# Performer attention layer, last batch: feature buffers of their own for two query groups, and a new order of the closing stages

## The reference, cut to what matters

```
feature_map(y): (exp(y @ orf.T / 32**0.25 - |y|^2 / (2 sqrt(32))) + 1e-6) / sqrt(128)    # per head, 16 heads of 32
q, k = feature_map(x Wq^T + bq), feature_map(x Wk^T + bk);   v = x Wv^T + bv
kv = k^T v;  ksum = sum over tokens of k;   out = (q kv) / (q ksum)
x = layernorm(x + out Wo^T + bo)
x = layernorm(x + x (ternary(weight) * scale)^T)
```

## Time and profile before

| | us |
|---|---|
| median of 3 runs | 1277.04 (1276.66 to 1277.28) |
| the profiled execution | 1281.79 |
| its span in the trace | 1280.0 |
| TensorE busy | 1257.8 (98%) |
| VectorE, ScalarE, GpSimd busy | 901.4, 712.4, 359.1 |
| mean granted TensorE clock | 0.996 of full speed |

### The profile page before, as it was taken

One profiled execution on the slowest core, in us unless ns is written; L12 is line 12 of the kernel. 1 busy time (PEld: TensorE's weight loads), 2 busy tenths in 40 slices (PEclk: granted clock), 3 DMA queues, 4 the chain that ended last, 5 costly groups with the idle time before them and its releaser, 6 DMA issues.

```text
span 1280.0 us, 24908 instructions
## 1 busy us (share of the span) xinstructions
PE 1257.8 (98%) x8626; PEld 961.0 (75%) x8626; DVE 901.4 (70%) x1615; ACT 712.4 (56%) x1435; POOL 359.1 (28%) x745
## 2 busy tenths in 40 slices
PE   9999999999999999999999999999999999999986
PEld 8767688777877678776787778876788777886665
DVE  6589665796658865688657877578765686657666
ACT  5657445574366743667337763477544674355534
POOL 0113342124321333213422134312342133421143
PEclk9999999999999999999999999999999999999899
DMA  7658304773146811576215761268603774046611
GB/s 240 152 135 216 97 34 122 178 197 83 54 118 170 209 54 58 139 178 175 62 58 139 193 166 55 62 157 203 158 25 85 173 191 130 34 114 143 152 34 66
DMA packets 82748, 160.32 MB, mean 125 GB/s; under 512 B 17856, under 2 KB 36416, under 8 KB 82112
## 3 DMA queue, kind: packets, MB, share of 16 engines
q1 hardware_dynamic: 68880, 139.78, 43.8%
q10 hardware_dynamic: 9648, 16.85, 3.5%
q0 software_dynamic: 4096, 2.11, 0.7%
HBM read 39.13 MB, written 16.78 MB: 44 GB/s over the span
## 4 chain that ended last, share of the span: by engine, by line
PE 88%; DVE 2%; ACT 1%; DMA 1%; issue 1%; SPq 1%; POOL 1%; ACTq 0%; POOLq 0%; DVEq 0%
PE ps L969 25%; PE ps L932 21%; PE ps L1033 9%; PE ps L982 8%; PE ps L987 5%; PE ps L1000 4%; PE ps L955 4%; PE ps L957 4%; PE ps L956 4%; PE ps L1059 2%; DMA rows<-in_x_t 1%; DMA stacks<-norm_rows 1%; PE ps L1009 1%; DVE stats L789 0%; SPq L534 0%
## 5 line engine op out<-in xcount | busy, mean ns | idle before, releaser
L691 ACT ACTIVATE features<-ps 128x512 f32<-128x512 f32 x512 | 277.8, 602 | 133.2 <-PE ps L982 127.3
L982 PEld LDWEIGHTS ps<-orf_stack,stacks 98*128 98x128 f32 x1024 | 131.3, 192 | 30.5 <-issue 21.3
L932 PE MATMUL ps<-Wo_hi,stacks 128*128 128x512 f32 x448 | 150.5, 402 | 0.0
L672 ACT ACTIVATE unit_hi<-ps,cols 128x512 fp32r<-128x512 f32 x128 | 88.5, 691 | 103.8 <-PE ps L969 103.8
L664 ACT ACTIVATE values_then_attention<-ps 128x512 f32<-128x512 f32 x64 | 38.2, 597 | 192.9 <-PE ps L957 190.8
L841 DVE SCALAR_TENSOR_TENSOR unit_lo<-ps,cols,unit_hi 128x512 fp32r<-128x512 f32 x128 | 94.0, 734 | 63.6 <-ACT squares L674 63.6
L583 POOL CAST norm_rows<-norms_turned 128x32 fp32r<-128x32 f32 x64 | 14.0, 219 | 439.9 <-DVE norms_turned L859 439.9
L805 DVE TENSOR_TENSOR den<-den,features 128x512 f32<-128x512 f32 x186 | 127.9, 688 | 11.5 <-ACT features L691 0.9
L982 PE MATMUL ps<-orf_stack,stacks 98*128 98x128 f32 x1024 | 130.9, 272 | 1.2 <-ACT features L691 1.1
L567 POOL TENSOR_SCALAR stats<-stats 128x1 f32<-128x1 f32 x128 | 36.0, 282 | 340.0 <-DVE stats L792 339.8
L1033 PE MATMUL ps<-features,kv_ksum 128*32 128x512 f32 x1024 | 123.1, 608 | 2.5 <-ACT kv_ksum L712 1.6
(11 more groups left out here) (132 smaller groups left out, 2598.6 us busy)
## 6 DMA issues: line engine op xcount, KB each, us to landing
stacks<-unit_hi SPq DMA_DIRECT2D x512, 128.0 KB, 2.4
stacks<-unit_lo SPq DMA_DIRECT2D x256, 128.0 KB, 2.7
out<-rows ACTq DMA_DIRECT2D x56, 256.0 KB, 2.0
rows<-in_x_t SPq DMA_DIRECT2D x49, 256.0 KB, 3.3
rows<-in_x SPq DMA_DIRECT2D x32, 256.0 KB, 4.0
features<-in_x SPq DMA_DIRECT2D x32, 256.0 KB, 3.7
values_then_attention<-in_x_t SPq DMA_DIRECT2D x8, 256.0 KB, 6.9
stacks<-norm_rows POOLq DMA_DIRECT2D x128, 16.0 KB, 2.6
```

The lines of the kernel that those rows point to most:

```text
L672: nc.scalar.activation(EH[:, u % 2, half], ps[:, :], ACT.Identity, bias=BC[:, u:u + 1]).then_inc(a_p.sem, 1)
L691: nc.scalar.activation(FE[:, n % 8, :, 0:M], ps[:, :].rearrange("p (a m) -> p a m", a=HG), ACT.Exp, scale=C_EXP).then_inc(a_exp.sem, 1)
L932: last = mm(out, a, b, start=(n == 0), stop=(n == len(terms) - 1))
L982: last = mm(ps[:, M * h:M * (h + 1)], slot[0:QK, L * h + P * r:L * h + P * (r + 1)], ORF[0:QK, h, :], start=True, stop=True)
```

## The change

It touches the last batch only. The query features of units 5 and 7 go to `own_buffers` (XR, X4, a new buffer of two tiles, and DR[:, 1]), not to FE. Unit 5 runs G2 ahead of F5.2 and P(7,1), and after F5.7 it goes F6.0, F6.1, GG2.0, GG2.1, R2.0, Q(7,1), N, LIFT, NL. Unit 6 has no G left. Unit 7 runs F7.0, F7.1, then all eight G3 tiles. All eight x rows load into FE once G3.7 is done. AG(0,1), AG(1,1), AG(2,1), A and GG3.1 move as shown. In the closing loop Y(t-1) stands ahead of ST(t-4), and SP issues the stores in place of ACT. `sums_on_pe` is unchanged.

```diff
 def split_at(b, g):
-    return 4 if sums_on_pe(b, g) else 0
+    return 0
+def has_own_buffers(b, u):
+    return b + 1 == B and u in (NU - 3, NU - 1)
...
     if is_key(u):
-        early = [("AG", b, 0, 0), ("AG", b, 1, 0)] if b + 1 == B and u + 2 == NU else []
+        if b + 1 == B and u + 2 == NU:
+            return f(2, 3, 4) + [("R", b, g - 1, 1), ("AG", b, 0, 0)] + f(5, 6, 7) + [("AG", b, 1, 0)]
...
         if b + 1 == B and u == NU - 3:
-            seq += p[1] + s0 + l0 + kv + f(2, 3) + p[2] + f(4, 5) + s1 + q0 + [("KVT", b, g)] + f(6, 7) + l1 + [("GG", b, g, 0)] + q1 + norm + lift
-            seq += [("GG", b, g, 1), ("R", b, g, 0)] + [("LR", b, t) for t in range(4)]
+            seq += kv + f(2, 3) + p[1] + [("KVT", b, g)] + q0 + f(4, 5) + p[2] + s1 + l1 + f(6, 7)
+            seq += [("F", b, u + 1, 0), ("F", b, u + 1, 1), ("GG", b, g, 0), ("GG", b, g, 1), ("R", b, g, 0)] + q1 + norm + lift
...
     if b + 1 == B:
-        seq = [("R", b, g - 1, 1), ("AG", b, 2, 0)] + f(0, 1, 2) + kv + [("AG", b, 0, 1)] + f(3) + [("OK", b, 0, 0)]
-        seq += [("KVT", b, g)] + f(4, 5) + [("AG", b, 1, 1), ("AG", b, 2, 1), ("A", b, 0), ("A", b, 1), ("OK", b, 0, 1), ("OK", b, 0, 2)]
-        seq += [("GG", b, g, 0), ("R", b, g, 0, 0), ("AG", b, g, 0, 0)] + f(6, 7) + [("OK", b, 1, k) for k in range(3)]
-        seq += [("R", b, g, 0, 1), ("AG", b, g, 0, 1), ("OK", b, 0, 3), ("LN", b, 0), ("OK", b, 1, 3), ("LN", b, 1), ("A", b, 2), ("A", b, 3)]
-        seq += [("GG", b, g, 1)] + [("OK", b, 2, k) for k in range(KT)] + [("LN", b, 2), ("Y", b, 0), ("A", b, 4)]
+        seq = f(0, 1) + kv + [("LR", b, t) for t in range(4)] + f(2, 3) + [("AG", b, 2, 0), ("OK", b, 0, 0), ("KVT", b, g)] + f(4, 5) + [("OK", b, 0, 1)] + f(6, 7)
+        seq += [("AG", b, 0, 1), ("OK", b, 0, 2), ("A", b, 0), ("A", b, 1), ("GG", b, g, 0), ("R", b, g, 0, 0), ("AG", b, g, 0, 0)]
+        seq += [("OK", b, 1, k) for k in range(3)] + [("R", b, g, 0, 1), ("AG", b, g, 0, 1), ("GG", b, g, 1)]
+        seq += [("OK", b, 0, 3), ("LN", b, 0), ("OK", b, 1, 3), ("LN", b, 1), ("AG", b, 1, 1), ("AG", b, 2, 1), ("A", b, 2), ("A", b, 3)]
+        seq += [("OK", b, 2, k) for k in range(KT)] + [("LN", b, 2), ("Y", b, 0), ("A", b, 4)]
...
-        seq += o(t, 3) + [("LN", b, t)] + (o(t + 1, 0, 1, 2) if t + 1 < TT else []) + [("YT", b, t - 2), ("ST", b, t - 4), ("Y", b, t - 1), ("FF", b, t - 3)]
+        seq += o(t, 3) + [("LN", b, t)] + (o(t + 1, 0, 1, 2) if t + 1 < TT else []) + [("YT", b, t - 2), ("Y", b, t - 1), ("ST", b, t - 4), ("FF", b, t - 3)]
...
+        own_buffers = [XR[:, r, :] for r in range(4)] + [X4[:, :], F2[:, 0, :], F2[:, 1, :], DR[:, 1, :]]
...
+                elif kind == "ST" and b + 1 == B:
+                    t = at[0]
+                    wait(a_out.sem, a_out.nth(b, t + 1))
+                    sp.dma_start(out_tiles[b, t], normed(b, t)).then_inc(d_st[t % 4].sem, 16)
```

More of the change, by code:

```diff
@@ L103, in unit_stages @@
         st = [[("ST", b - 1, t)] if u == 0 and b else [] for t in (TT - 2, TT - 1)]
-        half = [("G", b, g, r) for r in range(split_at(b, g))]
-        early = [("AG", b, 0, 0), ("AG", b, 1, 0)] if b + 1 == B and u + 2 == NU else []
+        if b + 1 == B and u + 2 == NU:
+            return f(2, 3, 4) + [("R", b, g - 1, 1), ("AG", b, 0, 0)] + f(5, 6, 7) + [("AG", b, 1, 0)]
         if u == 0:
-            seq = f(0, 1) + p[1] + s0 + l0 + f(2, 3) + q0 + st[0] + p[2] + f(4, 5) + half + s1 + l1 + f(6, 7) + q1 + norm + lift
+            seq = f(0, 1) + p[1] + s0 + l0 + f(2, 3) + q0 + st[0] + p[2] + f(4, 5) + s1 + l1 + f(6, 7) + q1 + norm + lift
             seq += st[1] + p[3]
         else:
-            seq = f(0, 1) + p[0] + s0 + l0 + f(2, 3) + p[1] + q0 + f(4, 5) + half + p[2] + early + s1 + l1 + f(6, 7)
+            seq = f(0, 1) + p[0] + s0 + l0 + f(2, 3) + p[1] + q0 + f(4, 5) + p[2] + s1 + l1 + f(6, 7)
             seq += ([("R", b, g - 1, 1)] if side_by_side(b, g - 1) else []) + q1 + norm + lift + p[3]
@@ L121, in unit_stages @@
         splits = xt(0) if u == NU - 3 else []
-        seq = p[0] + (s0 + l0 if b + 1 < B or u < NU - 3 else []) + splits + f(0, 1)
+        seq = p[0] + s0 + l0 + splits + f(0, 1)
         if u == 1 and b == 0:
@@ L283, in attention_kernel @@
         XR, X4 = sb("rows", [P, 4, D]), sb("fifth_x", [P, D])
+        F2 = sb("two_features", [P, 2, D])
         BO = sb("out_bias", [P, D])
@@ L386, in attention_kernel, with features_of @@
         s_w = [sem(f"setup_w_{w}") for w in "kqof"]
+        own_buffers = [XR[:, r, :] for r in range(4)] + [X4[:, :], F2[:, 0, :], F2[:, 1, :], DR[:, 1, :]]
+        def features_of(b, u, r):
+            if has_own_buffers(b, u):
+                return own_buffers[r].rearrange("p (a m) -> p a m", a=HG)
+            return FE[:, r, :, 0:M]
         staged_a = FE[:, 0:4].rearrange("p a h m -> p (a h m)")[:, 0:KT * D].rearrange("p (k o) -> p k o", k=KT)
@@ L417, in turned_rows, with x_rows @@
             return last_hi[:, t, :], last_lo[:, t, :]
-        def x_rows(t):
+        def x_rows(b, t):
+            if b + 1 == B:
+                return FE[:, t, :, 0:M]
             return XR[:, t, :].rearrange("p (a m) -> p a m", a=HG) if t < 4 else FE[:, t - 4, :, 0:M]
@@ L478, in load_rows @@
             def load_rows(b, t):
-                sp.dma_start(x_rows(t), x_tiles[b, t].rearrange("p (a m) -> p a m", a=HG)).then_inc(d_xr[t].sem, 16)
+                sp.dma_start(x_rows(b, t), x_tiles[b, t].rearrange("p (a m) -> p a m", a=HG)).then_inc(d_xr[t].sem, 16)
             for kind, b, at, _, _ in steps():
@@ L504, in _ @@
                     t = at[0]
-                    if t >= 4:
+                    if b + 1 == B:
+                        wait(t_g.sem, t_g.nth(b, 8 * NG))
+                    elif t >= 4:
                         wait(t_gg.sem, t_gg.nth(b, 2 * NG))
-                    elif b + 1 < B:
+                    else:
                         wait(*x_split(b + 1, t + 5 if t < 3 else t))
-                    else:
-                        wait(d_st[t].sem, d_st[t].nth(b, 0))
                     load_rows(b, t)
+                elif kind == "ST" and b + 1 == B:
+                    t = at[0]
+                    wait(a_out.sem, a_out.nth(b, t + 1))
+                    sp.dma_start(out_tiles[b, t], normed(b, t)).then_inc(d_st[t % 4].sem, 16)
                 elif kind == "LIFT":
@@ L612, in _ @@
                         pool.wait_ge(s_bo, 1)
-                    nc.gpsimd.tensor_tensor(x_rows(t), x_rows(t), BO[:, :].rearrange("p (a m) -> p a m", a=HG), ALU.add).then_inc(g_xb.sem, 1)
+                    nc.gpsimd.tensor_tensor(x_rows(b, t), x_rows(b, t), BO[:, :].rearrange("p (a m) -> p a m", a=HG), ALU.add).then_inc(g_xb.sem, 1)
                 elif kind == "LN":
@@ L682, in _ @@
                     v, r = u - 1, at[1]
-                    if u == 0:
+                    if has_own_buffers(b, u):
+                        if u == NU - 3 and r == 0:
+                            for sig in d_st:
+                                act.wait_ge(sig.sem, sig.nth(b, 0))
+                        elif u == NU - 3 and r == 4:
+                            act.wait_ge(*x_split(b, 4))
+                        elif u == NU - 1:
+                            act.wait_ge(t_gg.sem, t_gg.nth(b, u - 3 + r // 4 + 1))
+                        if r == 7:
+                            act.wait_ge(v_a.sem, v_a.nth(b, u - 1))
+                    elif b + 1 == B and u == NU - 2:
+                        act.wait_ge(t_g.sem, t_g.nth(b, 8 * (u // 2 - 1) + r + 1))
+                        act.wait_ge(v_ks.sem, v_ks.nth(b, 7 * (u // 2 - 1) + max(r, 1)))
+                    elif u == 0:
                         act.wait_ge(t_gg.sem, t_gg.nth(b, 0))
@@ L690, in _ @@
                         act.wait_ge(t_gg.sem, t_gg.nth(b, v - 1 + r // 4 + 1))
-                    nc.scalar.activation(FE[:, n % 8, :, 0:M], ps[:, :].rearrange("p (a m) -> p a m", a=HG),
+                    nc.scalar.activation(features_of(b, u, r), ps[:, :].rearrange("p (a m) -> p a m", a=HG),
                                          ACT.Exp, scale=C_EXP).then_inc(a_exp.sem, 1)
@@ L729, in _ @@
                     apply_norm(1, b, u)
-                    act.wait_ge(a_out.sem, a_out.nth(b, u + 1))
-                    act.dma_start(out_tiles[b, u], normed(b, u)).then_inc(d_st[u % 4].sem, 16)
+                    if b + 1 < B:
+                        act.wait_ge(a_out.sem, a_out.nth(b, u + 1))
+                        act.dma_start(out_tiles[b, u], normed(b, u)).then_inc(d_st[u % 4].sem, 16)
             for sig in d_st:
@@ L905, in _ @@
                         normed(b, u).rearrange("p (a m) -> p a m", a=HG), ps[:, :].rearrange("p (a m) -> p a m", a=HG),
-                        x_rows(u), ALU.add))
+                        x_rows(b, u), ALU.add))
                 elif kind == "YT":
@@ L1033, in _ @@
                             last = mm(bank[DH * h:DH * (h + 1), :], KVS[:, g % 2, c + DH * h:c + DH * (h + 1)],
```

(2 more changed lines are left out.)

2 lines of the change are left out of this document (1 added, 1 removed).

## The result

| | before | after |
|---|---|---|
| median, 4 runs each | 1276.88 us (1276.66 to 1277.28) | 1283.86 us (1283.01 to 1284.83) |
| the profiled execution | 1281.79 | 1284.83 |
| its span | 1280.0 | 1283.0 |
| mean granted TensorE clock | 0.996 | 0.993 |

The ratio is 1.005, 95% interval 1.0038 to 1.0063: the change costs 7.0 us. The forecast was 1278.7 with a range up to 1282.5, so the time lies outside it, on the side of the rival that said the clock falls at GG2 too.

What follows compares the result with a forecast made beforehand. TensorE, busy in 98% of the span, bounds the kernel, so only its stands could move the time. 0 - 0.1 + 2.1 + 2.2 - 1.0 + 0.9 - 2.4 = +1.7 on 1277.04 gave 1278.7 us, range 1273.0 to 1282.5.

Steps and rivals of the forecast that it cites:

- The clock falls at GG2 too: Rival: clock falls in GG2 despite the shorter stand, GG2.1's turn and N 2.6 us later, 1281.3 us; chance 0.25.
- Part 2: TensorE in GG2: clock stays full, GG2.1's denominators turn 2.6 us earlier, TensorE through with unit 6 at about 1208.9.
- The base: Profiled execution's 4.75 us above the median of the runs, carried over as a constant, giving 1277.04 us before the sum.
- Part 3: Norm rows of unit 7: N 3.3 us later, F7.0 at 1214.8 (-0.1), TensorE standing some 5.9 us before it.
- Part 1: Front of GG2.0: F5.0's exponential loses its 3.71 us wait, GG2.0 starts no earlier; 0, ends -1 and +0.7.
- Part 4: F7.0 to GG3.0: G3.0 to G3.3, 1.97 us, come on top, about 0.1 for F7.6 and F7.7; +2.1.
- Part 5: Behind the wait at F7.0: F7.0 and the first G run at 1.2 GHz; +2.2, ends 0 and 3.5.
- Part 6: GG3.0 to R3.1: GG3.0's denominators turned sooner, -1.0; GG3.1's turn ahead of LN(0), LN(2) waiting for A(2), +0.9.
- Part 7: Closing loop: with Y6 and Y7 issued earlier, YT6 and YT7 wait less; -2.4, ends 0 and -3.6.

Runs made afterwards that it cites:

- run 4: Changed kernel with the old tail (ST(t-4) ahead of Y(t-1), stores issued by ScalarE): 1287.36 us, ratio 1.0075.
- run 2: Changed kernel with idle matmuls in the two stands of GG2 (six ahead of F6.0, four ahead of GG2.1), norms left late: 1283.16 us, ratio 1.0044.
- run 3: Kernel before with only the changed tail (Y(t-1) ahead of ST(t-4), last batch's stores on SyncE): 1276.43 us, ratio 0.9988.
- run 9: Kernel before with the changed tail and idle matmuls, 7 ahead of GG2.0 and 4 ahead of GG2.1: 1274.59 us, ratio 0.9974.
- run 1: Changed kernel with unit 7's Q(7,1), N, LIFT and NL moved ahead of F6.0: 1278.85 us, ratio 1.0006.
- run 5: Changed kernel with unit 7's norms ahead of F6.0 and idle matmuls ahead of F6.0, GG2.1 and F7.0 (6, 4, 4): 1276.83 us, ratio 0.9992.
- run 6: Changed kernel with unit 7's norms early, idle matmuls in three front stands, and A(2), A(3) right behind AG(3,0,1): 1273.04 us, ratio 0.9964.
- run 11: Kernel before with the changed tail, idle matmuls ahead of GG2.0 and GG2.1, and A(2), A(3) right behind AG(3,0,1): 1273.47 us, ratio 0.9964.
- run 8: Changed kernel with G3.0 to G3.3 back in unit 6, ahead of F6.6, norm rows left late: 1280.07 us, ratio 1.0017.
- run 10: Changed kernel with unit 7's norms ahead of F6.0 and A(2), A(3) right behind AG(3,0,1), no idle matmuls: 1275.05 us, ratio 0.9976.
- run 7: Kernel before, old order and tail, with only the new buffers and all x rows loaded into FE behind G3.7: 1277.08 us, ratio 0.9994.

## Why the prediction was wrong

Two steps failed, part 2 in the profiled execution and the base in the medians.

**Part 2**, "I take it that the clock stays full". It fell in GG2.0, behind the stand of 1.34 us, as it had behind the old one of 1.61. The turn of GG2.1's denominators came 0.7 us later than before, counted from F5.0, where I had it 2.6 earlier. N and all of part 3 stand in VectorE's queue behind that turn, so F7.0 was 3.1 us later than I had it: 3.1 of the 4.2 us by which the sum missed the trace. (By its own terms GG2.1 would start at 1204.4 and not at 1204.25; that is 0.15 us of it.) In run 4's trace, where the clock does stay full in GG2, F7.0 comes 22.9 us behind F5.0, close to the 22.5 of the forecast, so the rest of parts 2 and 3 holds. The rival "The clock falls at GG2 too" named the mechanism and the decider. I gave it the smaller chance because waits in the tail had left the clock full; the experiments show that a trace in which it stays full says little of the next execution. But part 2 alone doesn't carry the miss: with the fall in GG2 gone from its trace, run 2 still measured 1283.16 us, above the range.

**The base.** I carried the 4.75 us between the profiled execution and the median over as a constant. It was not one. About 2.6 us of it is a loss at 100 to 150 us that no other trace here has: waits of TensorE of 1.12, 0.40 and 1.13 us, the last for a norm row, in a stretch where the slowest norm row DMA took the 6.9 us of the earlier trace rows to land. The other 2.1 us are, by the mean clocks, the fall in GG2 itself. Of the 69 executions of the kernel before in the experiments, 34 had a mean clock of 0.999 and a median of 1277.05 us, and 16 had 0.996, as its trace, and 1279.16. The median of before is thus, by this reading, a run without the fall, and the 2.6 us that part 2 took as a gain were not there to be gained in it. The four runs after lie at 0.992 to 0.994, each with more time at 1.2 GHz than before's. So the 5.9 us between the traces are 5.9 + 2.1 - 1.0 = 7.0 between the medians, the 1.0 being what the profiled execution after lies above its own median. That is by inference: only the traces show where the clock fell, and run 4's has a mean clock of 0.993 with GG2 at full speed. From traces the fall in the old front costs rather 2.7 us (runs 3 and 9, 85.44 and 82.75 us from F5.0 to the end).

Here is the stretch in the two traces, before and then after:

```profile
100.00:150.00 50.00, 47.27 (x378) 1.00 0.70 177
```
```profile
100.00:150.00 50.00, 49.90 (x391) 1.00 0.72 189
```

**Part 1** was right in its mechanism: the exponential's wait went, P(7,1) was late next, and GG2.0 started 0.4 us later from F5.0, inside the ends given.

**Part 3** was right but for what it inherited. From N to F7.0 I had 4.55 us; it took 4.36, and TensorE stood 5.49 us where I said 5.9. Run 1 shows the gate: with the norms early the wait is gone, and 0.0044 of the ratio with it (the stretch at 1.2 GHz behind the wait is in that sum). Both DMA issues took 1.09 us as in the earlier trace rows, with VectorE in an AG over two SBUF inputs at 1212.23. The rule that I weighed (the Trainium skill, SBUF — State Buffer, SBUF: two separate sides, the "DVE blocks DMA" trap) speaks of VectorE operations in a mode that uses two ports. I had left this condition out, and nothing here shows that AG is one, so my estimate of up to 0.7 us had no ground in it; this trace shows no such hold. F7.0 began 2.4 us behind the second issue (1212.61 by the 0.55 between the two), under the 2.6 that I took.

**Parts 4 and 5** were together +4.3 and measured +4.9. The clock behind the long stand was at 1.2 GHz until 1220.3, 5.2 us into the work and not 4.4. It had fallen 0.5 us into the stand, much sooner than at the end of the kernel before.

**Part 6**: -1.0 came as -0.98, and +0.9 as +1.3; the wait of LN(2) for A(2) grew to 2.04 us. I had seen that A(2) is late and took it for small. Runs 5 and 6 price it: 3.8 us in the new front, once the norms are out of the way, with the fall of the clock behind YT1's wait in that sum; in the old front, where YT1 waits 0.7 us, the early adds gave 1.1 (runs 9 and 11).

**Part 7**: -2.4 came as -2.3 in the trace, and run 3 shows the same 2.3 for the tail alone.

## What to carry to other kernels

When a change lets work go earlier on the engine that bounds, ask where the small chain that feeds its next stage stands in the other engines' queues: here 1.6 us of work on VectorE (two passes over the squares, and N), put behind the turn of GG2.1 and a division, held TensorE for 5.5 us. Fill a stand with the work that lies beside it rather than collect that work in one place: the four G3 tiles that left this place were 2 us of such work. And before a profiled execution is taken as the base, compare its mean clock with those of the other runs: what it shows may happen in a part of them only. A short stand leaves the clock to chance; behind the stand of 5.4 to 5.5 us it was at 1.2 GHz in all three traces that have one (after, runs 2 and 4).

## What the runs showed of the hardware

The clock falls behind stands far shorter than the 5.9 us that I had in mind, and not each time. In the traces of before, after and run 3 it fell in GG2.0, 0.7 to 1.7 us after TensorE had resumed behind a single stand of 1.34 to 1.61 us; the second stand, of 0.86 us, came only after that. With like stands (0.8 to 1.5 and 0.89 us) the clock stayed full in GG2 in runs 1, 4, 8 and 10 and fell 5 to 6 us behind the second stand: in run 8 at G3.0, behind a further stand of 0.92 us, in runs 1 and 10 about when F7.0 began, behind one of 0.9 us, and in run 4 at the start of the long stand. In run 7, with before's own stands, it did not fall there at all. With both stands filled and no long one behind them it did not fall at this place in any of the four traces (runs 5, 6, 9 and 11), and the mean clocks agree: 7 of run 3's 11 executions had 0.996, and none of run 9's seven was under 0.998.

The long stand didn't have to last for the clock to fall: it fell 0.5 us into it in the trace after, 0.2 in run 4's and 2.8 in run 2's, where the two stands ahead of it were filled. YT1's wait of 3.3 to 3.7 us came with 1.2 GHz in runs 1, 2, 4, 5 and 8, but not in the trace of the change itself, and what made the difference stays open; with a wait of 1.3 us or less there it stayed full in each trace (before and runs 3, 6, 7, 9, 10, 11).

Eleven matmuls of 128x128 whose results nobody reads thus seem worth 0.0014 of this kernel's time (runs 3 and 9, 1276.43 and 1274.59 us; the intervals just overlap, the traces differ by 2.7 us), on an engine that is busy for 98% of it.
